# In the gather loop, an item's token products run in the next step, directly behind that step's slice logits

## What is computed

```python
xn = layernorm(x)
# graph attention over the edges (src, dst)
h = xn @ W_layer.T + b_layer
v = leaky_relu(a1[src] + a2[dst]);  ev = exp(v - segment_max(v, src))
gnn = segment_sum(ev / segment_sum(ev, src)[src] * h[dst], src)
# linear attention over all nodes, 8 heads: q = elu(xn wq + bq) + 1, k likewise
mix = (q @ (k^T v)) / (q . sum k) @ wo + bo
x = x + gnn + mix
# slices: y = layernorm(x), 8 heads of 64 slices
sw = softmax((y @ W_x + b_x) @ W_slice / temp)        # slice weights, 512 a node
token = (sw^T @ (y @ W_fx)) / sum(sw)                 # over all nodes
out = x + (attention among tokens, spread back by sw) @ W_out + b_out
```

## Time and profile before

| | us |
|---|---|
| median of 3 runs | 2304.6 |
| lowest, highest run | 2302.0, 2306.59 |
| span of the profiled execution, its only time | 2306.1 |
| TensorE busy in it (matmul records) | 1454.6 |
| VectorE busy | 1270.9 |
| POOL busy | 1004.7 |
| ACT busy | 677.9 |

### The profile page before, as it was taken

The page is one execution under the profiler, slowest core; times in us unless marked ns, Lnnn a source line. Parts: engine busy times, 40 slices in busy tenths (PEclk is TensorE's granted clock), DMA queues, the critical chain, the costliest instruction groups (busy, mean ns, idle before and its releaser), DMA issues. The chain is left out here.

```text
span 2306.1 us, 27679 instructions
## 1 busy us (share of the span) xinstructions
PE 1454.6 (63%) x8420; PEld 1093.9 (47%) x8420; DVE 1270.9 (55%) x4043; ACT 677.9 (29%) x1884; POOL 1004.7 (44%) x1126
## 2 busy tenths in 40 slices
PE   5599995355745655655655656656646547465889
PEld 3477874234534434434434434434434435344667
DVE  8978783154644644644644545545545535445744
ACT  0243441042322322322322323323323323223310
POOL 1167676535445445445345345345344354453000
PEclk8799997577778877778878778778777777787999
DMA  8011213223223223223223222222232232221064
GB/s 178 29 47 48 62 50 90 71 58 88 70 70 87 69 69 86 69 73 84 68 73 83 68 76 80 68 77 79 65 83 77 62 87 68 69 77 55 14 193 153
DMA packets 112593, 177.17 MB, mean 77 GB/s; under 512 B 35998, under 2 KB 84509, under 8 KB 112445
## 3 DMA queue, kind: packets, MB, share of 16 engines
q0 software_dynamic: 43184, 109.96, 18.0%
q1 hardware_dynamic: 52847, 44.64, 7.5%
q10 hardware_dynamic: 16414, 20.81, 2.9%
HBM read 139.68 MB, written 35.65 MB: 76 GB/s over the span
## 5 line engine op out<-in xcount | busy, mean ns | idle before, releaser
L1134 POOL DMA_INDIRECT big<-node_table,rest x825 | 784.9, 951 | 239.9 <-issue 225.9
L1220 PE MATMUL psum<-big 128*125 128x257 f32 x1700 | 399.2, 388 | 39.4 <-DVE big L1757 39.1
L1220 PEld LDWEIGHTS psum<-big 128*125 128x125 f32 x1700 | 316.2, 191 | 93.9 <-DVE big L1757 46.1
L1575 DVE TENSOR_SCALAR rest<-psum,rest 128x125 f32<-128x125 f32 x100 | 30.1, 344 | 594.8 <-remote 554.1
L1239 PE MATMUL psum<-rest 65*125 65x512 bf16 x52 | 34.6, 666 | 488.6 <-ACT big L1376 488.6
L1132 POOL TENSOR_TENSOR rest<-rest 1x1 f32<-1x1 f32 x100 | 18.9, 189 | 693.7 <-PE psum L1220 668.0
L1370 ACT ACTIVATE rest<-big,rest 128x125 f32<-128x125 bf16 x850 | 268.9, 493 | 134.2 <-DVE rest L1705 134.2
L1239 PEld LDWEIGHTS psum<-rest 65*125 65x125 bf16 x52 | 9.2, 176 | 521.2 <-ACT big L1376 521.0
L1376 ACT COPY big<-psum 128x250 f32<-128x250 f32 x52 | 19.1, 367 | 687.1 <-remote 682.5
L1241 PE MATMUL psum<-rest,big 128*125 128x512 f32 x208 | 177.5, 1005 | 0.0
L1757 DVE TENSOR_SCALAR big<-big,rest 128x125 f32<-128x125 bf16 x850 | 169.0, 281 | 0.0
(11 more groups left out here) (430 smaller groups left out, 2786.7 us busy)
## 6 DMA issues: line engine op xcount, KB each, us to landing
big<-node_table,rest POOLq DMA_INDIRECT x825
slice_weights<-rest ACTq DMA_DIRECT2D x51, 252.0 KB
big<-slice_weights SPq DMA_DIRECT2D x50, 252.0 KB, 3.8
node_table<-big SPq DMA_DIRECT2D x50, 126.0 KB
normalised_turned<-big SPq DMA_DIRECT2D x50, 125.0 KB
rest<-normalised_turned SPq DMA_DIRECT2D x50, 125.0 KB
out_dram<-rest ACTq DMA_DIRECT2D x50, 125.0 KB
X<-in_x_dram SPq DMA_DIRECT2D x1, 5600.0 KB
```

Of the source, the lines that this page charges most:

```text
L1134: pool.indirect_dma_start(Gt[:, u, q * TW:(q + 1) * TW], None, table, bass.IndirectOffsetOnAxis(ap=item[:, u, 2 * q:2 * q + 1], axis=0)).t ...
L1220: mm = pe.matmul(bank[bAgg][0:R, 0:D + 1], P[:, u, q, :], Gt[:, at, q * TW:q * TW + D + 1], start=q == 0, stop=q == Q - 1)
```

## The change

In `step` of TensorE's gather loop, `tokens` is taken from between `turn_largest` and `queries` and put into the next step, behind `logits` and ahead of `norms`, with the y buffer of the step before. The first step has none (`first`). The last step of the loop has both: the one of the step before behind its logits, its own where it stood. The argument `n` of `tokens` wasn't used and is dropped. No instruction is added or taken away.

```diff
-                    def tokens(n, u, L=L, last=False):
+                    def tokens(u, L=L, last=False):
...
-                    def step(i, j, k, ahead, final=False):
+                    def step(i, j, k, ahead, final=False, first=False):
                         u, n, odd = j % U, 2 * k + j // U, j % 2
                         v, w, nv = (u + 1) % U, (u + 2) % U, n + 1 if u == U - 1 else n
                         spread(i)
                         logits(i)
+                        if not first:
+                            tokens((u - 1) % U)
                         norms(i + 1)
...
                             logits(i + 1, bF2, yT2)
-                            tokens(i, u)
+                            tokens(u)
                             return
-                        tokens(i, u)
                         if ahead:
                             queries(i + 2, w, nv)
...
                     for i in range(SURE):
-                        step(i, i % LU, i // LU, True)
+                        step(i, i % LU, i // LU, True, first=i == 0)
```

More of the change, by code:

```diff
@@ L1344, in _ @@
                     turn_weights(last, bF2, L2)
-                    tokens(last, TAIL % U, L2)
+                    tokens(TAIL % U, L2)
                     turn_weights(last + 1)
-                    tokens(last + 1, (TAIL + 1) % U, L, True)
+                    tokens((TAIL + 1) % U, L, True)
                     pe.wait_ge(sum_psum, last + 2)
```

## The result

| | before, us | after, us |
|---|---|---|
| median of 4 runs each | 2303.3 | 2347.2 |
| lowest, highest | 2292.7, 2306.6 | 2344.9, 2348.7 |
| span of the profiled execution | 2306.1 | 2346.9 |
| ratio after to before, 95% interval | | 1.0196 [1.0173, 1.0218] |

The change costs 44 us, against a forecast of 52. But the runs of the later sections met five chips, and on two of them the kernel before takes 1610 to 1613 us, not 2303, and there the change makes it 1% faster. Each chip was met in one series of runs only, so whether its kind stays isn't known.

The account below looks back on a forecast made before the run. A chain of waits through POOL's gathers and TensorE's release 3.1 us after them sets the step. 1.3 less 0.2 gives 1.1 us, times 47 is 52 us: 2358 for the profiled execution, 2356 median, range 2288 to 2392.

Parts of the forecast that it names:

- The ring: Step's loop of waits: gathers, TensorE's release 3.1 us after the last, work up to eight sums, next gathers; 35.25 us.
- The back part: TensorE's work released after the gathers: removing the token products there gains 0.2 us a step through earlier yT.
- The front part: From yT's release to the first eight sums: token products between logits and norms add 0.8 to 1.8 us, middle 1.3.
- Both paths: TensorE's norms and transposes, VectorE's subtraction and edge weights: each delays the first sums 0.8 to 1.8 us, VectorE's slightly later.
- the fast case: Token products behind the logits at full clock, records every 0.43 us: VectorE's subtraction comes 0.8 us later.
- the slow one: Token products behind the logits with one or two records at low clock: VectorE's subtraction comes 1.35 or 1.8 us later.
- rival (a): Slow clock for all four token records behind the logits: 2.6 us a step, 122 us, 2427 us; chance 0.10.
- The number of steps: The 47 places where ACT's yT copy waited for release, each 1.1 us longer: 52 us.
- Rival (b): No measurable change, within 0.2%: yT about 1 us early in most steps pays for the token products; chance 0.12.
- (c): Faster: early yT lets logits and token products run under the gathers, 14 us gained, 2291 us; chance 0.16.
- The extreme of (c): TensorE's queue drains before being held at all: some 11 us a step, 500 us in all, about 1790; chance 0.04.
- The forecast's sign: The whole kernel gets slower, by over 0.2% with chance 0.68; faster has 0.20.

Follow-up runs that it names:

- the last experiment: Kernel before with VectorE's weigh moved ahead of soft_below, on a chip of the slower kind: 2257.1 us, ratio 0.979 to the kernel before.

## Why the prediction was right, and where it was not

**The ring.** Right for the ordinary steps, on the kind of chip that it was read from. yT 3.1 us behind the last gather with the change as without it; four gathers fewer 260 us off for 235; plain loads, and the ring is gone. The sentence that it would fail "if the release turns out to depend on how much TensorE has queued" was put to the test by the change itself: four records fewer stood before the queries, these were complete 3.6 to 4.3 us sooner, and yT moved by 0.15 us. But the release isn't bound to the gathers' end as such: in 20 steps of the last experiment turn_y ends at most 4.4 us behind a pause in the gathers and is released within 0.4 us, with gathers running. In the ordinary steps turn_y's record ends some 9 us behind the first gather, 7.6 with the change, and is held in both. The early step of the kernel before is not explained by this: turn_y ends 8.7 us behind the first gather there and is released 7.2 us later.

**The back part.** Booked at 0.2 us a step, measured 0.15. The bounds for what the token products take there, 1.88 to 5.7 us, hold the measured 3.6 to 4.3.

**The front part.** Booked at 1.3 us, between 0.8 and 1.8. The first sum starts 1.09 us later after 16 gathers and 1.58 after 17, 1.34 in the mean. Both paths were named rightly: norms move by 1.81 or 2.49 us and it costs less, because they run fast then; the subtraction waits for the token products by 1.1 to 1.6 us. The parts of the two kinds of step were the wrong way round: the forecast had the fast case (+0.8) after 17 gathers and the slow one (+1.35 to +1.8) after 16. Measured, two records are slow after 17 gathers, the longer pause of TensorE, and less than one after 16. That the mean fits is in part luck. The mechanism of rival (a) is in this spread: two slow records of four at most, not four.

**The number of steps.** The term that was mis-sized. The forecast took 47 steps of 1.1 us, 52 us. From the first to the last item's gathers the loop became 40.9 us longer (485.0 to 2095.1 us before, 481.5 to 2132.6 after). The first 37 of these 46 steps took 40.7 us of it, 1.10 each; the last nine took 324.3 us before and 324.6 after. The clock tells why. In four of these nine the kernel before ran its first sums partly on the low clock: sixteen of them took 4.0 to 5.0 us, for 3.36 elsewhere. With the change they took 3.36 in all but one of the nine. One pair of steps, at the same place of the loop, before (norms and transposes, then the sums) and after (the sums), columns as in the earlier trace rows:

```profile
1941.00:1944.40 3.40, 3.27 (x22) 2.73 (x21) 3.26 (x13) 3.14 (x10) 0.00 (x0) 0.50 0.01 2
1944.40:1950.80 6.40, 6.35 (x25) 5.27 (x26) 5.93 (x26) 4.71 (x12) 1.27 (x2) 0.84 0.03 3
```

```profile
1984.00:1990.00 6.00, 5.94 (x29) 4.94 (x30) 5.54 (x27) 4.74 (x13) 1.18 (x3) 1.00 0.03 3
```

The way from yT to the next gathers is 13.25 us before and 13.22 after in this pair. Where the clock rises only during the sums, the token products ahead of them take up slow time that the sums would have had, and the sums give it back. These four steps became 2.6 us shorter together, the other five 2.9 us longer. Why the clock rises later in those steps of before than in the first 37 wasn't tried.

**Rival (b) and (c)** needed an earlier yT. It moved by 0.15 us. The argument against them, that an early yT gains little because the exponents are bound to the same point, came from one step. The last experiment has an early yT in nearly every second step, and there the exponents start from 2.6 us before to 1.9 us behind the last gather's end, not 3 us behind it. That little is gained is right; the reason was another, the pause of the gathers and the low clock of the sums.

**The extreme of (c)**, a hold that is absent from the whole loop, is nearest to what two of the five chips do, with or without the change: 1595 to 1613 us, with steps of 21. No row with gathers could have told that. The forecast's sign holds for the slower kind of chip, and the reverse was measured on the other: there the front part waits for VectorE, and the token products fill that wait. The 1.95 us ahead of the norms in the steps without gathers, which the prediction used as cover for the last steps, was the one row that showed such a step.

## What to carry to other kernels

Find out what an engine's stage is released by before pricing its move: under the gathers the token products held up the work behind them by some 4 us, and taking them out gained 0.15 us; behind the release the same products, 1.88 us at full clock, cost 1.34 us a step. Look at the steps of a loop in which the suspected cause is absent; they show what the kernel does without it, and here what it does on another chip. A change of 1 or 2% may have another sign on another chip of the same type, so that a gain is worth a second chip before it is believed.

## What was unexpected in the hardware

- The same program took 2288 to 2307 us on three of five chips, and 2303 us in the runs shown first, and 1610 to 1613 us on the other two. The runs of one comparison agree within 1.5%.
- On the slower ones, completions of TensorE are raised late while GpSimd issues gathers: 4 to 15 us after the records' ends, with yT released 3.1 us after the last gather ends, after 16 or 17 of them. Up to 4.7 us behind an item's first gather they are still raised within 0.3 us (kernel before), and behind a pause of 1.6 to 2.1 us in the gathers turn_y's is raised within 0.4 us (20 steps of the last experiment). With the same transfers issued by SyncE the delay is absent (2307 to 1620 us on one chip). The Trainium skill (SBUF — State Buffer, SBUF: two separate sides) says that engine ports and DMA ports can't contend with each other. The plain loads agree with it: with the same bytes landing, TensorE is not held. The 687 us are lost between TensorE and GpSimd's gathers; which resource is held wasn't found.
- The gathers themselves look alike on both: in the mean 949 ns a record of the changed kernel in the runs shown first, and 970 on the faster kind of chip.
